# A graph network on one core: the last step of a layer put in another order on TensorE, and the first phase's radial loads issued by ScalarE

## What is computed

```python
# phase 0, equivariant message passing
x1  = silu(radial @ W1 + b1); x2 = silu(x1 @ W2 + b2); w = x2 @ W3 + b3   # per edge, 8 -> 64 -> 64 -> 256
msg = products of x[src] (8 scalars, 8 vectors) with the edge's 4 harmonics and w
x   = layernorm(x + x @ Wself + segment_sum(msg, dst) / 4)
# three spline convolutions; 64 taps of 32x32, 8 of them weigh on each edge
for l in 1, 2, 3:
    msg = sum over 8 corners: basis[e, s] * (x[src] @ W_l[tap(e, s)])
    x   = batchnorm(leaky(segment_sum(msg, dst) / count + x @ R_l + b_l) + x)   # no leaky in the third
out = layernorm(x1 + x)
```

## Time and profile before

| | us |
|---|---|
| median of 3 runs | 14115.63 (14110.87 to 14133.57) |
| the profiled execution | 14111.41, its span 14109.6 |
| phase 0, POOL's first gather to its last | 24 to 3991 |
| busy in that stretch | PE 3392, DVE 3244, POOL 3015, ACT 877 |
| end of phase 0 and start of layer 1 | 3991 to 4105 |
| one layer's 98 steps | 3225 to 3237 |
| PE busy in the 3225 us of layer 1 | 3098 |
| from one layer's steps to the next | 102 to 104 |

### The profile page before, as it was taken

One profiled execution on the slowest core, in us unless ns is written; L12 is line 12 of the kernel. 1 busy time (PEld: TensorE's weight loads), 2 busy tenths in 40 slices (PEclk: granted clock), 3 DMA queues, 4 the chain that ended last, 5 costly groups with the idle time before them and its releaser, 6 DMA issues.

```text
span 14109.6 us, 239107 instructions
## 1 busy us (share of the span) xinstructions
PE 12868.3 (91%) x75547; PEld 9687.5 (69%) x75547; DVE 10949.8 (78%) x16519; ACT 7811.7 (55%) x14096; POOL 10540.3 (75%) x10542
## 2 busy tenths in 40 slices
PE   7888888888889999999989999999997999999997
PEld 3444444444458888888867888888886888888885
DVE  7888888788877777777777777777777777777777
ACT  1222222222247777776756777777775777777775
POOL 7777777777767777777767777777775777777775
PEclk9999999999989999999999999999998999999998
DMA  2111111111111111111111111111111111111111
GB/s 50 22 23 21 22 22 21 22 22 22 21 39 31 33 33 31 33 33 31 33 40 33 31 33 33 31 33 33 31 33 40 31 33 33 31 33 33 31 33 41
DMA packets 941460, 434.99 MB, mean 31 GB/s; under 512 B 681631, under 2 KB 894076, under 8 KB 941120
## 3 DMA queue, kind: packets, MB, share of 16 engines
q0 software_dynamic: 339456, 186.75, 8.8%
q1 hardware_dynamic: 431032, 217.76, 5.7%
q10 hardware_dynamic: 170888, 29.48, 1.1%
HBM read 396.32 MB, written 36.84 MB: 31 GB/s over the span
## 4 chain that ended last, share of the span: by engine, by line
PE 40%; POOL 25%; DVE 15%; issue 13%; DMA 6%; SPq 1%; DVEq 0%; ACT 0%; POOLq 0%; ACTq 0%
POOL xg L620 25%; PE ps L1763 21%; PE ps L1746 9%; DMA xg<-x_rows,idx 4%; PE ps L1656 3%; DVE big L1421 2%; DVE R L1139 2%; DVE big L1106 2%; DVE big L1115 2%; PE ps L1673 2%; PE ps L1610 1%; DVE big L1229 1%; DVE xg L1425 1%; DVE big L1117 1%; PE ps L1766 1%
## 5 line engine op out<-in xcount | busy, mean ns | idle before, releaser
L620 POOL DMA_INDIRECT xg<-x_rows,idx x7329 | 7435.2, 1014 | 2357.0 <-issue 2081.3
L1763 PE MATMUL ps<-x_high,row_hot 128*128 128x512 f32 x12276 | 5054.9, 412 | 393.2 <-DVE big L1421 376.6
L1763 PE MATMUL ps<-x_low,row_hot 128*128 128x512 f32 x12276 | 4864.5, 396 | 0.0
L869 ACT ACTIVATE row_hot<-row_of,window_ids 128x256 fp32r<-128x256 f32 (+1 forms) x8232 | 3194.5, 469 | 1292.6 <-PE ps L1766 1292.6
L620 POOL DMA_INDIRECT xg<-in_x,idx x3125 | 3014.7, 965 | 975.9 <-issue 961.6
L1763 PEld LDWEIGHTS ps<-x_high,row_hot 128*128 128x128 f32 x12276 | 2347.3, 191 | 1090.3 <-DVE big L1421 398.0
L1421 DVE TENSOR_TENSOR big<-ps,col_hot 128x512 f32<-128x512 f32 x2058 | 1421.4, 691 | 1929.0 <-DMA xg<-x_rows,idx 1112.9
L1763 PEld LDWEIGHTS ps<-x_low,row_hot 128*128 128x128 f32 x12276 | 2352.2, 192 | 433.7
L1746 PE MATMUL ps<-big 128*128 128x128 f32 x18816 | 2399.0, 281 | 10.9 <-DVE big L1431 10.9
L1746 PEld LDWEIGHTS ps<-big 128*128 128x128 f32 x18816 | 2205.5, 193 | 13.0 <-DVE big L1431 13.0
L913 ACT COPY big<-ps 128x1024 f32<-128x1024 f32 x1176 | 1187.8, 1010 | 1163.4 <-PE ps L1746 1134.3
(11 more groups left out here) (161 smaller groups left out, 10261.0 us busy)
## 6 DMA issues: line engine op xcount, KB each, us to landing
row_of<-pick_rows SPq DMA_DIRECT2D x294, 448.0 KB
xg<-x_rows,idx POOLq DMA_INDIRECT x7329, 2.4
xg<-in_x,idx POOLq DMA_INDIRECT x3125, 2.4
carry<-carry_items SPq DMA_DIRECT2D x392, 48.0 KB
agg_rows<-rts ACTq DMA_DIRECT2D x294, 64.0 KB
meta<-in_coord_t SPq DMA_DIRECT2D x294, 48.0 KB
big<-in_rad SPq DMA_DIRECT2D x196, 64.0 KB, 3.0
idx<-in_src_t SPq DMA_DIRECT2D x392, 16.0 KB
```

The lines of the kernel that those rows point to most:

```text
L620: return nc.gpsimd.indirect_dma_start(out=dst_tile, out_offset=None, in_=table, in_offset=bass.IndirectOffsetOnAxis(ap=index, axis=0))
L869: far = nc.scalar.activation(hot[:, :, b, :], row_of[:, par, ks.start:ks.stop, :], ACT.Abs, bias=window_ids[:, b:b + 1], scale=-1.0)
L1763: nc.tensor.matmul(ps[:, bank, :], row_hot[:, half, at, b, :], x_part[:, b * ROW:b * ROW + ROW], start=(b == 0 and n == 0), stop=False)
```

## The change

Two edits. In phase 0, the loads of `rad` for all steps but the first leave SP's queue; ACT issues each one ahead of the silu of an odd part, when its wait for that part's first-layer matmul is over: behind part 1 half 0 of the next step, behind part 3 half 1 of it. In ACT's numbering parts 3 to 6 are issued inside step i, so part 5 brings half 0 of step i+2. To keep the step numbers in range, ACT's loop over pairs ends one pair sooner and the rest is written out.

In a layer, during the last step (97) all four parts of the taps of step 96 are issued behind chunk 2, ahead of the sums of chunk 3. After the step, the taps of step 97 come ahead of the totals of step 96: they wait for the scan of 96 (`R_ready`) in place of the copy of its totals, and the copy they wait for is that of step 95.

```diff
-            def load_radials(i, half):
-                if due(i):
-                    sp.wait_ge(h1_ready[1], 2 * i - 1 + half)
-                sp.sem_inc(loads_go, 1)
-                sp.dma_start(rad[0:2 * MUL, half], radials_of(rad_table[ds(i * STEP + 16 * half, 16), :])
-                             ).then_inc(rad_loaded[half], 16)
...
                 load_carry(i - 1, 1 - par, 0 if early and i < 3 else i - 2)
-                load_radials(i, 0)
-                load_radials(i, 1)
...
+            def next_radials(i, f):
+                half, step = f // 2 % 2, i + (f + 3) // 4
+                if isinstance(step, int) and step >= STEPS:
+                    return
+                act.dma_start(rad[0:2 * MUL, half], radials_of(rad_table[ds(step * STEP + 16 * half, 16), :])
+                              ).then_inc(rad_loaded[half], 16)
+
             def first_layer(i, f):
                 act.wait_ge(h1_ready[f % 2], 2 * i + f // 2 + 1)
+                if f % 2:
+                    next_radials(i, f)
...
-            with act.Fori(2, whole_pairs(2, STEPS - 1), 2) as i:
+            with act.Fori(2, whole_pairs(2, STEPS - 3), 2) as i:
...
-                    pe.wait_ge(rt_out, (l + 1) * STEPS + i)
+                    if last:
+                        pe.wait_ge(R_ready, (l + 1) * STEPS + i)
+                    pe.wait_ge(rt_out, (l + 1) * STEPS + i - last)
...
-                    if with_taps and ch >= chunks // 2:
+                    if with_taps and ch >= chunks // 2 and more:
                         for t in range(8 // chunks):
                             tap_products(l, i - 1, 1 - par, 8 // chunks * (ch - chunks // 2) + t)
+                    if with_taps and ch == chunks // 2 and not more:
+                        for t in range(4):
+                            tap_products(l, i - 1, 1 - par, t)
...
-                totals_by_cell((l + 2) * STEPS - 2)
                 for t in range(4):
-                    tap_products(l, STEPS - 1, (STEPS - 1) % 2, t)
+                    tap_products(l, STEPS - 1, (STEPS - 1) % 2, t, last=path.narrow)
+                if path.narrow:
+                    totals_by_cell((l + 2) * STEPS - 2)
                 totals_by_cell((l + 2) * STEPS - 1)
```

More of the change, by code:

```diff
@@ L444, in sync_program @@
             coord_table = a["coord_t"] if path.narrow else meta_items[:, :, 0:3, :]
-            rad_table = a["rad"] if path.narrow else rad_items
             in_frame, in_pairs = (slice(3, 4), slice(4, 5)) if path.narrow else (slice(3, 5), slice(3, 5))
@@ L519, in sync_program @@
                 sp.wait_ge(w3_ready, 2)
-                load_radials(0, 0)
+                for half in range(2):
+                    sp.sem_inc(loads_go, 1)
+                    sp.dma_start(rad[0:2 * MUL, half], radials_of(rad_items[16 * half:16 * half + 16, :])
+                                 ).then_inc(rad_loaded[half], 16)
                 load_indices(0, 0, 0, 0)
                 load_indices(0, 1, 1, 0)
-                load_radials(0, 1)
                 load_meta(0, 0, 0, sh_table, 5, META, in_frame)
@@ L751, in scalar_program @@
                     copy_block(b)
+            rad_table = a["rad"] if path.narrow else rad_items
+            if not path.narrow:
+                act.wait_ge(rad_stored, 16 * path.blocks)
+            def next_radials(i, f):
[3 more added lines that the diff above has]
+                act.dma_start(rad[0:2 * MUL, half], radials_of(rad_table[ds(step * STEP + 16 * half, 16), :])
+                              ).then_inc(rad_loaded[half], 16)
             def first_layer(i, f):
                 act.wait_ge(h1_ready[f % 2], 2 * i + f // 2 + 1)
+                if f % 2:
+                    next_radials(i, f)
                 if due(4 * i + f):
@@ L811, in scalar_program @@
                 l0_rows(i)
-            for i in range(whole_pairs(2, STEPS - 1), STEPS - 1):
+            for i in range(whole_pairs(2, STEPS - 3), STEPS - 1):
                 goes_row(i - 1, (i - 1) % 2, 0, 2 * ((i + 1) // 2))
@@ L1769, in pick_products, with tap_products @@
                 tr.then_inc(pick_done, 1)
-            def tap_products(l, i, par, t):
+            def tap_products(l, i, par, t, last=False):
                 if t == 0:
                     pe.wait_ge(s_out[3], layer.chunks // 4 * (l * STEPS + i + 1))
-                    pe.wait_ge(rt_out, (l + 1) * STEPS + i)
+                    if last:
+                        pe.wait_ge(R_ready, (l + 1) * STEPS + i)
+                    pe.wait_ge(rt_out, (l + 1) * STEPS + i - last)
                 for c in range(4):
```

## The result

The changed kernel takes 14068.5 us (median of 7 runs, 14059.9 to 14073.7), the kernel before 14110.9 (7 runs); the ratio is 0.9967, 95% interval 0.9956 to 0.9978. 14068 was forecast. The profiled execution has a span of 14069.4 us, 40.2 less than before. These rows of the profile after answer to the earlier trace rows: waits of phase 0 (total, times, longest), then the group of POOL's gathers.

The account below looks back on a forecast made before the run. POOL's gathers were taken to bound phase 0, PE the layers. From 14111.4 us, -6 (phase end), -28 (gathers' length) and -12.5 (layer ends) gave 14064.9; +3 for the median made 14068, range 14038 to 14104.

Parts of the forecast that it names:

- the sum: Whole kernel: -6 for phase 0's end, -28 for shorter gathers, -12.5 for the layer ends, together -46.5 us.
- The 3 us added for the median: Whole kernel: 3 us added to the profiled execution's forecast of 14064.9 us, giving 14068 for the median.
- What bounds: Phase 0: POOL's gathers, issued back to back with 0.30 us gaps, are the bound; PE's 491 us radial wait is slack.
- ScalarE's radial loads: Phase 0: 194 loads issued by ACT, at most 0.6 us each, delaying a silu; costed at nothing.
- (a) The end of phase 0: Last step of phase 0: DVE has caught up, so the third quarter starts at 3996.1 rather than 4002.24; -6 us.
- (b) The gathers' length: Phase 0: features begin where they stretch gathers by 0.02 us, not 0.10; one-hot rows unchanged; -28 us.
- the view's 2.4 us of landing: Phase 0: features begin 2.4 us plus 0.05 behind a quarter's last gather, around a slot's start, where they cost nothing.
- The slower rival: Phase 0: landings at 2.30 to 2.36 us put features at the dearest place; 40 us slower, 14155; chance 0.05.
- (c) PE's clock: Phase 0: PE's low clock level still comes, but 6 to 8 us of slack a step covers it; cost 0.
- Edit 2: Layer ends: earlier scan of step 96 gives 4.7, 4.7 and 3.1 us; swapping taps and totals gives 0; -12.5 us.

Follow-up runs that it names:

- the runs with fewer gathers: The kernel before and the changed kernel, each with 24 of 32 gathers a step in phase 0: 13654.9 us and 13645.3 us.
- edit 1 alone: The kernel before with ScalarE issuing the radial loads of phase 0, the layers' last step as before: 14077.8 us, ratio 0.9978.
- the kernel of the section on the two halves: The changed kernel with the taps of step 97 again behind the totals of step 96: 14074.0 us, ratio 0.9970 to the kernel before.
- the long reduction: The changed kernel with a VectorE reduction of 896 elements between the wait for a quarter's gathers and its features in phase 0: 14087.9 us.
- edit 2 alone: The kernel before with only the new order in each layer's last step, SyncE issuing the radials as before: 14095.8 us, ratio 0.9992.
- SP in another order: The kernel before with SyncE itself issuing a step's radial loads ahead of the next step's indices, layers as before: 14071.7 us, ratio 0.9976.

## Why the prediction was right

The time came within 1 us of the forecast, and that is luck; the mechanism is what was right. The profiled execution was forecast at 14064.9 us and took 14071.2. The stretches that the sum speaks of gave 50.4 us where it had 46.5, and the layers' steps, which it left out, took 10.9 back. The 3 us added for the median rested on three runs (14115.6); seven have a median of 14110.9.

*What bounds.* Right as read: POOL's gaps are the same to 0.2 us, and the runs with fewer gathers show the large wait to be slack. ScalarE's radial loads cost nothing, as put: its 194 issues take 0.33 us each by the median, 0.38 at most, and PE's waits for silu ahead of the second layer are 3.3 us against 2.9.

*(a) The end of phase 0.* -6 predicted, -6.4 measured. The third quarter of the last step begins at 3967.12, 9.85 us behind the second, which waited for its landing.

*(b) The gathers' length.* -28 predicted, -28.5 measured, but its two terms were off and the errors cancelled: that is luck too. The features were to give 28 and gave 19; the one-hot rows were to give 0 and gave 9. The step that failed is the start within the slot. I took the view's 2.4 us of landing plus 0.05, 2.45 us behind the last gather. The trace has a median landing of 2.36 us in both kernels, and the features begin 0.02 us behind it, so at some 2.37 us (1.12 us into the next slot, where I had put the slot after it). That is 0.02 to 0.04 us from the dearest place: features begun at 1.0 to 1.1 us (about 100 of the 374) stretch the next gather by 0.11 on average, those at 1.1 to 1.2 (about 185) by 0.02. For the same reason the one-hot rows began at 0.72 and not 0.8. The slower rival was nearer than its 0.05 said. It asked for landings of 2.30 to 2.36 us and put the dearest place 1.08 to 1.11 us into a slot; the features at 3957.27 above begin 1.07 us behind the gather at 3956.20, and the next gather takes 1.14 us, 0.20 more, as in the earlier trace rows. The size isn't firm either: with the same phase 0, the changed kernel twice, edit 1 alone and the kernel of the section on the two halves start their last gather at 3961.4, 3964.8, 3961.3 and 3956.4, 25 to 34 us before that of the kernel before.

The prediction read from one row that a gather is held until 1.30 us behind the start of the features, wherever it began. In the trace of the kernel before this holds for features begun at 0.94 to 1.08 us. Begun at 0.83 us, they have the next gather end 1.53 us behind their start, begun at 0.5 us, 1.84 us.

*(c) PE's clock.* Cost 0 predicted and found. POOL's gaps didn't grow, so PE never held it up. The granted clock of phase 0, as a share of 2.4 GHz, rose from 0.92 (24 to 3991) to 0.97 (24 to 3950), with short waits for DVE (356 of them, 1.6 us on average) in place of 95 for radials of 5.2 us.

*Edit 2.* -12.5 predicted for the ends; -15.3 in the profile after and -10 to -15 in the eight that have it. From the last `xm` to the scan of 96 the three layers gave 4.8, 3.9 and 3.3 us, 12.0 in sum for the 12.5 of the first half. The other 3.2 us came behind that scan, where I had put 0: 2.4 of them in layer 1, where the taps took 1.93 us instead of 3.64 and the totals of step 96 1.08 instead of 1.92, at the upper level of the clock.

*What the sum left out.* The layers' steps took 9714 us before and 9725 after, and nothing in the change touches them; it took 11 of the 51 us that the parts make. The other profiles speak against the change as the cause. The kernel with the long reduction has the changed kernel's layers and takes 9716; the kernel before with 24 gathers has the old ones and takes 9731. By chip, which is on record for all but the profiles before and after, it is 9708 to 9716 us in the four on chip 15 (edit 1 alone, edit 2 alone, SP in another order, the long reduction) and 9724 to 9736 in the seven on chips 5, 12 and 13. The medians of the kernel before go the same way: 14109 us on chip 15, 14115 to 14118 on the others. That the chip makes this difference isn't shown, since no kernel is known to have a profile on both sides of it, and on one chip, too, sums differ by up to 10 us. Single layers differ by up to 12 us between kernels whose layer code is the same, and no wait in them stands out; this stays open.

## What to carry to other kernels

A long wait on an engine that isn't the bound is a reading of the bound's pace: before spending an edit on it, look whether the engine named in the chain ever pauses. If it doesn't, the only gains are the pipeline's end and the length of the bound's own instructions. Busy shares don't name the bound: in phase 0 before, PE (3392 us) and DVE (3244) were busier than POOL (3015), whose 0.30 us behind each gather count as idle. In a queue, put loads that wait for little ahead of those that wait for much; another engine isn't needed for that.

## What the runs showed of the hardware

VectorE instructions with two inputs in SBUF make a GpSimd gather longer by 0 to 0.5 us, depending on when in the gather's slot they begin. A reduction from SBUF doesn't, and neither do products with an input in PSUM: 1041 gathers of the changed kernel beside such products alone have a median of 0.944 us and take 0.956 at most. Putting the features off by 0.2 us took 14 us from one stretch and gave 16 to another. The Trainium skill (SBUF — State Buffer, "Who interferes with whom") says that two SBUF inputs contend with GpSimd's reads and that a reduction never contends on this chip; the runs agree, with 0.94 us for the gather beside the 1.09 us reduction. In the same place it infers that such two-input instructions leave the making of DMA descriptors alone, which is not how the prediction had it. Here the gather's instruction gets longer, by 0.20 us at 3957.45 above; but a gather also reads its offsets (`idx`) out of SBUF, and which of the two is held up no run here shows.
